# Vector work of a gather stage moved between engines, a sixth gather buffer, and a re-timed step order in a four-stage transformer kernel

## What is computed

```python
x = _layernorm(x + _L0_attn_ref(x, ...))   # linear attention with decay, 8 heads
x = _layernorm(x + _L0_ffn_ref(x, ...))    # 2 layers: local attention (window 64), gated FFN
x = _layernorm(x + _L1_attn_ref(x, ...))   # wave attention: gathers
x = _layernorm(x + _L1_ffn_ref(x, ...))    # 8 experts, top 2
...
# _L1_attn_ref, per token l, sample s (33) and head h:
pos = clip(l + s_idx * freq_avg + phase_avg, 0, Ll - 1); lo = floor(pos); hi = min(lo + 1, Ll - 1)
g = x[lo] + frac * (x[hi] - x[lo])
out[l, h] = sum_s g[s, h] * w[l, h, s];   out = silu(out @ out_w.T)
...
# _L1_ffn_ref: softmax over the tokens, top 2 of 8 experts for each token
y = relu(relu(relu(x @ w1 + b1) @ w2 + b2) @ w3 + b3)    # for each expert
v = einsum('ebso,bse->eo', y, w_tok);  out = einsum('bse,eo->bso', ind, v)   # w_tok, ind: the gating
```

## Time and profile before

| | |
|---|---|
| median of 3 runs (lowest to highest) | 2073.46 us (2072.62 to 2075.66) |
| the profiled execution | 2070.78 us |
| its span | 2068.8 us |
| instructions | 30902 |
| PE / DVE / POOL / ACT busy | 1579.8 / 1315.5 / 1139.2 / 970.9 us |
| mean granted TensorE clock | 0.894 |
| indirect gathers | 1056, 1079.3 us on POOL |
| HBM read / written | 150.93 MB / 8.92 MB |

### The profile page before, as it was taken

How to read it: one execution, slowest core, us unless ns; L and a number is a source line. 1 busy time by engine, 2 the same in 40 slices (tenths; PEclk the granted TensorE clock), 3 DMA queues, 4 the chain that set the end, 5 groups by cost and what they waited for, 6 DMA issues and landing times. The chain is left out here.

```text
span 2068.8 us, 30902 instructions
## 1 busy us (share of the span) xinstructions
PE 1579.8 (76%) x11633; PEld 1023.0 (49%) x11641; DVE 1315.5 (64%) x2234; ACT 970.9 (47%) x2357; POOL 1139.2 (55%) x1137
## 2 busy tenths in 40 slices
PE   5687777777788867777878676778786559999856
PEld 3344343445554544455545444555454337677635
DVE  6676573678777746778778557887784353343345
ACT  3266565334545654345455542454655224343423
POOL 0000002777776637677776376777773747777720
PEclk8899898899999988899999898999999669999976
DMA  4010002333433334233333242333333523333311
GB/s 141 6 27 16 11 22 42 101 92 111 115 101 99 103 67 104 83 114 113 105 100 103 72 99 82 115 113 109 99 108 64 152 75 95 100 107 103 102 34 41
DMA packets 92374, 178.15 MB, mean 86 GB/s; under 512 B 21434, under 2 KB 49220, under 8 KB 91972
## 3 DMA queue, kind: packets, MB, share of 16 engines
q0 software_dynamic: 50688, 138.48, 24.2%
q1 hardware_dynamic: 41540, 37.70, 6.4%
HBM read 150.93 MB, written 8.92 MB: 77 GB/s over the span
## 5 line engine op out<-in xcount | busy, mean ns | idle before, releaser
L719 POOL DMA_INDIRECT pool_c<-rows_of_x,idx x1056 | 1079.3, 1022 | 494.9 <-issue 335.9
L1224 DVE TENSOR_TENSOR pool_c<-pool_c 128x768 f32<-128x768 f32 x352 | 333.8, 956 | 217.8 <-DMA pool_c<-rows_of_x,idx 212.5
L1599 PE MATMUL c<-ident,pool_c 128*128 128x128 f32 x2112 | 320.6, 294 | 108.7 <-DVE pool_c L1224 107.7
L1599 PEld LDWEIGHTS c<-ident,pool_c 128*128 128x128 f32 x2112 | 261.7, 151 | 202.7 <-DVE pool_c L1224 142.1
L703 POOL MEMSET pool_a<- 128x2048 f32 x4 | 7.2, 1806 | 343.8 <-PE ta L1529 343.7
L860 ACT ACTIVATE prob<-sc,nmax 128x128 f32<-128x128 f32 x512 | 179.3, 375 | 0.3 <-issue 0.2
L1499 PE MATMUL pa<-wqkv,pool_a 128*128 128x512 f32 x192 | 117.4, 696 | 22.6 <-DVE pool_a L1181 14.6
L771 ACT COPY pool_a<-tb 128x512 f32<-128x512 f32 x188 | 113.2, 602 | 44.5 <-PE tb L1380 42.4
L1499 PE MATMUL pb<-wqkv,pool_a 128*128 128x512 f32 x192 | 114.5, 681 | 17.2 <-DVE pool_a L1181 10.9
L860 ACT ACTIVATION_READ_ACCUMULATOR prob<-sc,nmax 128x1 f32 x512 | 110.5, 216 | 0.0
L1128 DVE TENSOR_REDUCE ssq<-pool_a 128x16 f32<-128x1024 f32 x64 | 77.8, 1215 | 46.3 <-ACT pool_a L836 45.8
(11 more groups left out here) (417 smaller groups left out, 3284.3 us busy)
## 6 DMA issues: line engine op xcount, KB each, us to landing
pool_c<-rows_of_x,idx POOLq DMA_INDIRECT x1056
vmix<-vring SPq DMA_DIRECT2D x128, 128.0 KB
rows_of_x<-x2tok SPq DMA_DIRECT2D x16, 256.0 KB
xtok<-in_x SPq DMA_DIRECT2D x4, 512.0 KB, 4.4
x_of_all<-x2tok SPq DMA_DIRECT2D x8, 256.0 KB, 2.5
out<-pool_c SPq DMA_DIRECT2D x8, 256.0 KB, 2.3
wqkv<-in_wqkv SPq DMA_DIRECT2D x1, 1536.0 KB
xtok<-x_of_all SPq DMA_DIRECT2D x3, 512.0 KB, 4.7
```

Source lines behind the costliest of these rows:

```text
L719: pool.indirect_dma_start(gat[:, n % GB, s, :], None, table, bass.IndirectOffsetOnAxis(ap=idx[:, t, SC * c + s:SC * c + s + 1], axis=0),). ...
L1224: V.tensor_tensor(g4, g4, wv, ALU.mult).then_inc(SEM["c_prod"], 1)
L1599: ins = mm(out[:, c:c + P], x, ident[:], start=(i == 0 and k == 0), stop=(i == BCH - 1 and k == len(parts) - 1), is_transpose=True, skip_g ...
```

## The change

The change does seven things:

- The weight products w (64 instructions of 128 x 264) go from GpSimd to VectorE, at the same place in the step order.
- The clearing of `vp` (4 instructions of 128 x 2048) goes from GpSimd to VectorE.
- There are two row tables, used by turns; the table write of batch b waits for the products of batch b-2. Filling the second table's fixed part adds two start-up loads.
- GB is 6: six gather buffers.
- The experts run batch by batch (q is batch, expert, half), vs comes 5 groups behind h1 where it was 3, and the gatings' steps are dealt among them at places listed in GATING_0 and GATING_AT.
- SyncE's loads for the experts are a step of their own at the tail's start.
- The tables of times have new numbers.

```diff
-GB = 5
+GB = 6
...
-PERIOD = 27.61
-TAIL_AT = 22.13
+FIRST_AT = (0.0, 27.61, 55.22, 82.83)
+SECOND_AT = (0.0, 27.61, 55.22, 82.83)
+TAIL_AT = 21.94
...
-HEAD_AT = ((17.62, 17.69, 17.86, 18.17, 18.18, 18.28, 18.29), (20.87, 21.07, 21.39, 21.99, 23.72, 25.33))
+HEAD_AT = ((17.93, 17.99, 18.0, 18.13, 18.14, 18.21, 19.38), (21.23, 21.24, 22.92, 23.7, 24.34, 25.36))
...
+GATING_0 = (1, 3, 12)
+GATING_AT = (16, 18, 22, 24, 30, 36, 50)
...
     if q < QE:
-        e, k = divmod(q, EARLY * J)
-        return e, k // J, k % J
+        m, k = divmod(q, E_ * J)
+        return k // J, m, k % J
...
-    beside = [s for m in range(EARLY) for s in gating_steps(m)] + moe_steps(0, QE, ("h1", "h2", "y", "vs"))
-    beside += [("x3T", EARLY, 0), ("lg", EARLY, 0)] + moe_steps(QE, QL, ("h1", "h2", "y"))
+    products = {"h1": 0, "h2": 1, "y": 2}
+    beside = gating_steps(0)[:4]
+    for i, step in enumerate(moe_steps(0, QE, {**products, "vs": 5})):
+        beside.append(step)
+        m, k = divmod(i, 4 * E_ * J)
+        if m == 0 and k in GATING_0:
+            beside.append(gating_steps(0)[4 + GATING_0.index(k)])
+        if m + 1 < EARLY and k in GATING_AT:
+            beside.append(gating_steps(m + 1)[GATING_AT.index(k)])
...
-                    wait(sp, "c_prod", b, 0)
+                    table = tables[b % 2]
+                    if b > 1:
+                        wait(sp, "c_prod", b - 1, 0)
...
-                if what == "zero":
-
-                    wait_filled(pool, ("O", LAYERS - 1, T - 1), b - 1)
-                    nc.gpsimd.memset(vp[:], 0.0).then_inc(SEM["a_zero"], 1)
+                pass
...
-                        gat[:, n % GB, s, :], None, table,
+                        gat[:, n % GB, s, :], None, tables[b % 2],
...
-                    for c in range(2):
-                        ins = nc.gpsimd.tensor_tensor(
-                            wlh[:, t % 2, :, c, :], ap3(wk[:, t, 2 * H:], [[1, S], [S, H]]),
-                            ap3(frac[:, S * t:, c], [[2, S], [0, H]]), ALU.mult)
-                    ins.then_inc(SEM["c_w"], 1)
...
+                if what == "zero":
+
+                    wait_filled(dve, ("O", LAYERS - 1, T - 1), b - 1)
+                    V.memset(vp[:], 0.0).then_inc(SEM["a_zero"], 1)
...
+                elif what == "w":
+
+                    t, = a
+                    wait(dve, "c_pos", b, 13 * (t // TB + 1))
+                    wait(dve, "c_prod", b - (t < 2), NCH * (t - 1 + (T if t < 2 else 0)))
+                    for c in range(2):
+                        ins = V.tensor_tensor(
...
-        for at in (0, D):
-            out_.append((v["table"][BLK:N + 1, at:at + D], dram["x"][0, 0:N + 1 - BLK]))
+        for i in range(2):
+            for at in (0, D):
+                out_.append((v["tables"][i][BLK:N + 1, at:at + D], dram["x"][0, 0:N + 1 - BLK]))
```

More of the change, by code:

```diff
@@ L156, in schedule @@
     for b in range(B):
-        out += [(PERIOD * b + time, ("first", b, *step)) for time, step in first_times(e)]
-        out += [(PERIOD * b + time, ("second", b, *step)) for time, step in second_times() if b < B - 1 or time < TAIL_AT]
+        out += [(FIRST_AT[b] + time, ("first", b, *step)) for time, step in first_times(e)]
+        out += [(SECOND_AT[b] + time, ("second", b, *step)) for time, step in second_times() if b < B - 1 or time < TAIL_AT]
     return [step for _, step in sorted(out, key=lambda x: x[0])] + tail_steps()
@@ L214, in moe_steps @@
     out = []
-    for q in range(q0, q1 + len(stages) - 1):
-        for lag, what in enumerate(stages):
+    for q in range(q0, q1 + max(stages.values())):
+        for what, lag in stages.items():
             if q0 <= q - lag < q1:
@@ L237, in tail_steps @@
     second = [("second", B - 1, *x) for x in late + [x for x in second_steps() if x not in late] if x not in done]
[L238 to L240 removed]
+    products = {"h1": 0, "h2": 1, "y": 2}
[7 more added lines that the diff above has]
+            beside.append(gating_steps(m + 1)[GATING_AT.index(k)])
+    beside += [("x3T", EARLY, 0), ("lg", EARLY, 0)] + moe_steps(QE, QL, products)
+    last = moe_steps(QL, QA, products)
     behind = [("x3T", EARLY, 1), ("lg", EARLY, 1)] + last[:3] + [("soft", EARLY), ("rank", EARLY)]
@@ L252, in tail_steps @@
     k = len(second) - CLEAR
-    return second[:h] + merge(second[h:k], [("moe", B, *x) for x in beside]) + second[k:] + [("moe", B, *x) for x in behind]
+    return [("moe", B, "load")] + second[:h] + merge(second[h:k], [("moe", B, *x) for x in beside]) + second[k:] + [("moe", B, *x) for x in behind]
 FIRST_KEYS = {
@@ L480, in build @@
         tri = pool_c[:, 8 * N:8 * N + P]
-        table = nc.dram_tensor("rows_of_x2", (N + 1, 2 * D), F32, kind="Internal").ap()
+        tables = [nc.dram_tensor(f"rows_of_x2_{i}", (N + 1, 2 * D), F32, kind="Internal").ap() for i in range(2)]
         x3_dram = nc.dram_tensor("x3_of_all", (B * N, D), F32, kind="Internal").ap()
@@ L657, in moe @@
             def moe(what, *a):
-                if what == "x3T" and a == (0, 0):
+                if what == "load":
                     load_x3(0)
```

24 lines of the change are left out of this document (11 added, 13 removed), and 6 rows, old and new, of the table AT.

## The result

The changed kernel takes **1982.34 us** (median of 4 runs, 1979.33 to 1988.94) where the kernel before took 2073.04 in the same comparison: ratio 0.9571, 95% interval 0.9553 to 0.9588. The prediction was 1998 us with a range of 1955 to 2052.

The account below looks back on a forecast made before the run. Periods were taken as bound by the dependent chain of "first" through TensorE, VectorE and ScalarE, GpSimd late in places; the tail is a gather stage. 2068.8 + 4.0 - 3 - 45 - 31 = 1993.8 us span, median 1998, range 1955 to 2052.

Parts of the forecast that it names:

- Start, +4.0 for the loads: Before the first gather: two more table fills delay the load TensorE's vu waits for by 4.0 us; bounds 0 and 6.
- Gathers earlier and the sixth buffer, -15 a period: Periods: GpSimd's lighter list and one chunk more run-ahead remove 15 of VectorE's 21.0 us gather waits; ends 0 and 29.1.
- Seam, -5 a period: Between batches: pos before co removes 6.7 us, gathers start some 10 us earlier; 5 of TensorE's 9.46 us back.
- That sign: Seam, GpSimd's gap between gathers: near 12 us expected, or still over 20 if the chain lags.
- VectorE's additions, +5 a period: Periods: weight products 6.8 and clearing 2.2 us make 9.0 us on VectorE, 5 on the path; ends 0 and 9.
- Tail, -31: Tail: buffer waits 27.2 and products 12.9 us leave GpSimd's path, 9 given back for TensorE; ends -15 and -40.
- Only the tail gives: Rival: the chain of "first" alone sets the periods, which gain nothing; tail -31, 2043 us; chance 0.20.
- VectorE's list becomes the path: Slower rival: VectorE's 9 us all lie on the chain, each period grows by 12, 2082 us; chance 0.06.
- Periods give nearly all: Rival: TensorE's 29.1 us product waits go, VectorE's additions fall into idle time, periods 27 shorter; 1962 us; chance 0.20.
- The change does not act: Rival: TensorE bounds the tail, the chain the periods; only the start's +4 shows, 2077 us; chance 0.03.
- The port rule: Tail: moved two-SBUF-input products on VectorE each hold a gather 0.43 us, 6.8 us in all; 2005 us; chance 0.05.
- The general link: Gathers: 1.04 us with VectorE 71% busy, 0.96 at 39%; 9 us more work adds some 1.6 us a batch, hidden.

## Why the prediction was right, point by point

- **The sum** gave 1993.8 us of span; the profiled one is 1986.9. The start came out 7.2 us below its terms, the three periods together 10.8 us below theirs (-18.6 us on the mean for -15), the tail 11 us above. So it is partly luck that the sum is only 7 us off: the tail's miss and the periods' cancel. The median, 1982.3, is further from the 1998 forecast, since the profiled execution is 6.6 us above the median, and since the 4.7 us between span and median were too many: an execution takes 2.0 us more than its own span (2070.78 to 2068.8, 1988.94 to 1986.9), and the rest compared a median with another execution's span.
- **Start, +4.0 for the loads: right**, 3.0 us with the old times, and TensorE's vu 3.6 us later in the changed kernel (30.80 for 27.22). What was missing is a term for the opening's new times, -9.2 us. I had costed the re-timing only at the seams.
- **Gathers earlier and the sixth buffer, -15 a period: the mechanism was right.** VectorE's wait for gathers went from 21.0 to 4.5 us in period 2; with five buffers it is 12.9 us, and the kernel takes 29.3 us more.
- **Seam, -5 a period: right in its first part.** The 6.7 us between sum and pos are gone, and came back with the old times. From the end of the last product to the first gather it is 13.5 us, and was 17.9. But TensorE's stall behind ScalarE is 7.88 us where I expected 4, and the gap in GpSimd's list 21.4 where I expected 12. That sign was badly chosen: the gap starts at the last gather, and GpSimd's last gather now comes 7.9 us before the last product, not some 4. The transposes' wait for x, up to 4.65 us, was in no term: the load is behind co, which was moved behind pos.
- **VectorE's additions, +5 a period: not shown by itself.** The products take 0.62 us for my 0.43 (between the bounds of 0.43 and 0.81), the clearing 1.77 for 2.2, 11.7 us a batch for 9.0. Against it stand the stretched instructions, which give back some 16.8 us in the whole run and which I had not seen in the trace of before. In period 2 VectorE is busy only 4.3 us longer. As the kernel with the products back on GpSimd is slower by 27.8 us, VectorE's cost is below what the move frees; how much of it lies on the path no run shows.
- **Tail, -31: the term that was wrong by most**, -20 measured. GpSimd's buffer waits fell as predicted, 27.2 to 6.9 us. But the 12.9 us of products were counted in full beside them, and taking them back to GpSimd costs 4.8 us there. TensorE is busy 303.3 us in the tail before and 301.6 in the changed one, up to the last gather; only its idle time, 70 us, could shrink, and it shrank by 19. The 9 us that I took back for TensorE were too few. TensorE is busy 75% of the first 100 us, where I had said over 80.
- **Rivals.** "Only the tail gives" fell with the periods. "VectorE's list becomes the path" fell: no period lengthened. "Periods give nearly all" came close in period 1 (-28.4) and not in the others. "The change does not act" fell with both. The port rule was right in its mechanism and too high in its size: VectorE's two-input instructions do hold gathers up, but beside the moved products that is at most 3.3 us in the tail for the 6.8 us reckoned, and the mean of all gathers is 1044 ns with the products on either engine. The general link that the prediction weighed, longer gathers where VectorE is busier, goes by the kind of instruction: beside those with at most one SBUF input gathers take 949 to 951 ns.

## What to carry to other kernels

When two engines share a stage through a ring of buffers, lighter work on the one, more buffers and an earlier start of the dependent chain pay together: the four parts taken back one by one cost more in sum than the whole change gains. When steps are moved past each other, follow the DMAs that wait for the moved step: the load of x behind co took back up to 4.65 us a seam, and in the kernel that issues it one step earlier that wait is gone. Before moving a product off GpSimd, look in the trace for instructions of VectorE that are longer beside it: that is part of the gain. And before reading a small effect, see whether the stage still waits for what was changed: where GpSimd waited 107 us a period for buffers, its load and its buffers could not count.

## What was not expected of the hardware

- Two VectorE products of 128x512 with both inputs in SBUF took 3.03 us beside a GpSimd pair of 1.54 us, and 1.3 us elsewhere; one of 128x1024 took 2.84 us beside a pair of 1.56 us, and 1.22 us elsewhere.
- Gathers that began while VectorE ran an instruction with two SBUF inputs took 1203 ns on the mean, 251 of 401 over 1 us; all others took 946 to 949 ns on the mean, 8 of 655 over 1 us (changed kernel).
- TensorE's busy time for the same period went from 313.0 to 325.7 us with the mean granted clock between 0.93 and 0.90, the product of the two within 1%; of the 11.6 us that taking the products back costs in period 1, 6.2 are TensorE's busy time (319.2 for 313.0 us).
- In other comparisons of the same kernel it took 13 to 14% longer. In the five-buffer kernels compared, the start before the first gather was as long as ever (339.6 and 340.8 us) and the first period was not (490.2 and 399.9 us). Kernels that carry the change with work added gained 0 to 0.6% there; the changed kernel itself was not run. The figures of this document hold for the comparisons in which the kernel before takes 2071 to 2073 us.
